# Attention with a fourth score bank, and the maxima in two slots of 1024 and 512 columns

## What is computed

```python
# in the feed-forward block, twice: T = 2048, 16 heads of 8 channels
scores = jnp.einsum('bqhd,bkhd->bhqk', q, k) / jnp.sqrt(jnp.float32(Dh))
attn = jax.nn.softmax(scores, axis=-1)
ctx = jnp.einsum('bhqk,bkhd->bqhd', attn, v).reshape(Bb, Ss, Dd)
# the latent attention, with weights that are folded to q, k, v first
attn = jnp.where(causal[None, None], attn, -jnp.inf)
attn = jax.nn.softmax(attn, axis=-1)
```

## Time and profile before

| | us |
|---|---|
| median of 3 runs | 3145.35 (3127.97 to 3156.62) |
| the profiled execution, own time | 3132.53 |
| its span, first to last instruction | 3130.8 |
| PE busy | 2834.4 (91%) |
| DVE busy | 1998.1 (64%) |
| ACT busy | 1757.0 (56%) |
| mean granted clock of PE | 0.910 |

### The profile page before, as it was taken

How to read it: one execution, slowest core, us unless ns; L and a number is a source line. 1 busy time by engine, 2 the same in 40 slices (tenths; PEclk the granted TensorE clock), 3 DMA queues, 4 the chain that set the end, 5 groups by cost and what they waited for, 6 DMA issues and landing times. The chain is left out here.

```text
span 3130.8 us, 49981 instructions
## 1 busy us (share of the span) xinstructions
PE 2834.4 (91%) x15208; PEld 1329.6 (42%) x15208; DVE 1998.1 (64%) x2708; ACT 1757.0 (56%) x3373; POOL 260.3 (8%) x488
## 2 busy tenths in 40 slices
PE   6788857999999998999499999958999999998998
PEld 2688853333333333444244444424333333334443
DVE  5544456888888882322567777636888888882222
ACT  4222210788787887443156666631788788786433
POOL 1222202000000000000211111111000000000000
PEclk9888855999999999899679998975999999998999
DMA  1000002111001100211211111111011111000211
GB/s 38 1 0 0 0 1 74 28 28 27 24 17 27 27 21 1 78 44 40 74 28 42 27 41 36 26 54 34 16 27 27 27 27 26 16 20 15 68 60 34
DMA packets 37077, 94.13 MB, mean 30 GB/s; under 512 B 9258, under 2 KB 23044, under 8 KB 28804
## 3 DMA queue, kind: packets, MB, share of 16 engines
q1 hardware_dynamic: 33892, 91.18, 10.8%
q10 hardware_dynamic: 3104, 1.88, 0.2%
HBM read 78.45 MB, written 13.76 MB: 29 GB/s over the span
## 5 line engine op out<-in xcount | busy, mean ns | idle before, releaser
L507 DVE TENSOR_REDUCE Hmaxes<-Hm 128x1 f32<-128x1024 f32 x512 | 603.2, 1219 | 100.4 <-PE Hm L271 99.0
L507 DVE TENSOR_REDUCE Fmaxes<-Fm 128x1 f32<-128x1024 f32 x512 | 603.2, 1219 | 99.8 <-PE Fm L271 98.3
L418 ACT ACTIVATE Hprob<-Hs 128x512 f32<-128x512 f32 x1024 | 528.7, 603 | 117.7 <-PE Hs L283 117.2
L418 ACT ACTIVATE Fprob<-Fs 128x512 f32<-128x512 f32 x1024 | 528.6, 603 | 117.8 <-PE Fs L283 117.3
L283 PE MATMUL Hs<-Hqa,Hka 64*128 64x512 f32 x1024 | 409.4, 467 | 5.6 <-ACT Hprob L418 5.1
L283 PE MATMUL Fs<-Fqa,Fka 64*128 64x512 f32 x1024 | 408.9, 466 | 5.7 <-ACT Fprob L418 5.1
L418 ACT ACTIVATE Lprob<-Ls 128x512 f32<-128x512 f32 (+3 forms) x640 | 301.8, 535 | 135.1 <-PE Ls L283 131.4
L271 PE MATMUL Hm<-Hka,Hqa 64*128 64x512 f32 x1024 | 351.2, 462 | 19.5 <-DMA Hka<-H_kparts 15.9
L271 PE MATMUL Fm<-Fka,Fqa 64*128 64x512 f32 x1024 | 350.6, 460 | 19.2 <-DMA Fka<-F_kparts 15.6
L271 PEld LDWEIGHTS Hm<-Hka,Hqa 64*128 64x128 f32 x1024 | 162.6, 195 | 277.2 <-DVE Hmaxes L507 253.2
L271 PEld LDWEIGHTS Fm<-Fka,Fqa 64*128 64x128 f32 x1024 | 162.3, 195 | 276.7 <-DVE Fmaxes L507 252.8
(11 more groups left out here) (450 smaller groups left out, 2962.6 us busy)
## 6 DMA issues: line engine op xcount, KB each, us to landing
Fqa<-F_qparts SPq DMA_DIRECT2D x64, 128.0 KB
Fka<-F_kparts SPq DMA_DIRECT2D x64, 128.0 KB
FEwb<-FE_weights SPq DMA_DIRECT2D x8, 1024.0 KB, 5.9
Lqa<-L_qparts SPq DMA_DIRECT2D x64, 128.0 KB
Lka<-L_kparts SPq DMA_DIRECT2D x64, 128.0 KB
Hqa<-H_qparts SPq DMA_DIRECT2D x64, 128.0 KB
Hka<-H_kparts SPq DMA_DIRECT2D x64, 128.0 KB
HEwb<-HE_weights SPq DMA_DIRECT2D x8, 1024.0 KB, 5.9
```

Of the source, the lines that this page charges most:

```text
L418: nc.scalar.activation(prob[:, kt % PSLOTS, q0:q1], seat(kt, n)[:, 0:q1 - q0], ACT.Exp, scale=SCALE).then_inc(expd, 1)
L507: nc.vector.reduce_max(maxes[:, qt, half:half + 1], mps[j % 2][:, 0:width], AX.X)\
```

## The change

PSUM's eight banks are divided anew. The ring of scores has four banks in place of three (`HIGH_SLOTS`). The slots for maxima are no longer two of 1024 columns but one of 1024 and one of 512 (`LOW_WIDTHS`), three banks in place of four. Items still alternate between the two slots, and an item is now as wide as its slot, or as the keys that are left. So a full attention has 48 items per head (16 of 1024 and 32 of 512 columns) and the causal one 32; the number of items is kept even by splitting the last one. `EARLY` goes to 12 items in both. A head's entries of the ring (66 and 42) are no multiple of four, so a seat depends on the parity of the head, and ACT's loop runs over pairs of heads.

```diff
-EARLY_FULL, EARLY_CAUSAL = 8, 9
+EARLY_FULL, EARLY_CAUSAL = 12, 12
+HIGH_SLOTS = 4
+LOW_WIDTHS = (2 * BANK, BANK)
...
-    MAXES = [(qt, half, min(2 * BANK, keys(qt) - 2 * BANK * half))
-             for qt in range(NT) for half in range(2) if keys(qt) > 2 * BANK * half]
+    MAXES = []
+    for qt in range(NT):
+        k0 = 0
+        for n in range(NB):
+            if k0 < keys(qt):
+                width = min(LOW_WIDTHS[len(MAXES) % 2], keys(qt) - k0)
+                MAXES.append((qt, n, k0, width))
+                k0 += width
+    if len(MAXES) % 2:
+        qt, n, k0, width = MAXES.pop()
+        MAXES += [(qt, n, k0, width - 2 * P), (qt, n + 1, k0 + width - 2 * P, 2 * P)]
...
-        return offset % 3
+        return offset % HIGH_SLOTS
...
-        maxes = sbo("maxes", [P, NT, 2], F32)
+        maxes = sbo("maxes", [P, NT, NB], F32)
...
-                    sp.sem_inc(expd, 3)
+                    sp.sem_inc(expd, HIGH_SLOTS)
...
-            sps = [ctx.enter_context(nc.psum_tensor(f"{name}s{i}", [P, BANK], F32)) for i in range(3)]
-            mps = [ctx.enter_context(nc.psum_tensor(f"{name}m{i}", [P, 2 * BANK], F32)) for i in range(2)]
+            sps = [ctx.enter_context(nc.psum_tensor(f"{name}s{i}", [P, BANK], F32)) for i in range(HIGH_SLOTS)]
+            mps = [ctx.enter_context(nc.psum_tensor(f"{name}m{i}", [P, w], F32)) for i, w in enumerate(LOW_WIDTHS)]
...
-            def seat(kt, n=0):
+            def seat(u, kt, n=0):
 
-                return ring(AHEAD[kt] + n + (kt > OUT_AFTER) + (kt > TURN_AT))
+                return ring(u * NE + AHEAD[kt] + n + (kt > OUT_AFTER) + (kt > TURN_AT))
...
-                        qt, half, width = MAXES[j]
+                        qt, _, k0, width = MAXES[j]
...
-                        k0 = 2 * BANK * half + n * BANK
+                        k0 += n * BANK
...
-                    head(0, first=True)
-                    with act.Fori(1, NH) as h:
-                        head(h)
+                    head(0, 0, first=True)
+                    head(1, 1)
+                    with act.Fori(1, NH // 2) as i:
+                        for u in range(2):
+                            head(i * 2 + u, u)
```

More of the change, by code:

```diff
@@ L100, in slot_of @@
     def slot_of(offset):
[L101 removed]
+        return offset % HIGH_SLOTS
     stream = [(1, j) for j in range(EARLY, NM)] + [(2, j) for j in range(EARLY)]
[L104 removed]
+    done = np.cumsum([120 + MAXES[j][3] for _, j in stream])
     length = np.cumsum([T - first_query(kt) + 300 * len(blocks(kt)) + (1500 if causal else 0) for kt in range(NT)])
@@ L282, in score @@
                         pe.wait_ge(expd, entry(h, kt, n) + 1)
-                        nc.tensor.matmul(seat(kt, n)[:, 0:q1 - q0], ka[0:LOW, s, kt * P:(kt + 1) * P],
+                        nc.tensor.matmul(seat(s, kt, n)[:, 0:q1 - q0], ka[0:LOW, s, kt * P:(kt + 1) * P],
                                          qa[0:LOW, s, q0:q1], start=True, stop=True).then_inc(scored, 1)
                     def weigh(h, s, kt):
-                        pe.wait_ge(expd, 3 + entry(h, kt, len(blocks(kt)) - 1) + 1)
+                        pe.wait_ge(expd, HIGH_SLOTS + entry(h, kt, len(blocks(kt)) - 1) + 1)
                         if causal:
@@ L325, in deliver @@
                         for j in range(NB):
-                            last = nc.tensor.transpose(ring(OUT_SEAT)[:, j * P:(j + 1) * P],
+                            last = nc.tensor.transpose(out_seat(u)[:, j * P:(j + 1) * P],
                                                        osb[:, j * P:(j + 1) * P] if source is None else source, ident)
@@ L339, in low_item @@
                     def low_item(h, i, s, j):
-                        for n in range(-(-MAXES[j][2] // BANK)):
+                        for n in range(-(-MAXES[j][3] // BANK)):
                             maxima(h, i, s, j, n)
@@ L358, in head @@
                             items = [(ahead, j) for ahead, j in share[kt] if ahead <= rest]
-                            low = [(ahead, j, n) for ahead, j in items for n in range(-(-MAXES[j][2] // BANK))]
+                            low = [(ahead, j, n) for ahead, j in items for n in range(-(-MAXES[j][3] // BANK))]
                             high = len(blocks(kt))
@@ L370, in head @@
                             if kt == OUT_AFTER:
-                                deliver(h, source=ident if first else None)
+                                deliver(h, u, source=ident if first else None)
                             if kt == TURN_AT:
-                                turn(turn_entry(h), TURN_SEAT, h + 2 if rest else h + 1)
+                                turn(turn_entry(h), turn_seat(u), h + 2 if rest else h + 1)
                     head(0, 0, first=True)
@@ L411, in _, with head @@
                                              ACT.Copy).then_inc(expd, 1)
-                    def head(h, first=False):
+                    def head(h, u, first=False):
                         for kt in range(NT):
@@ L491, in item @@
                     def item(h, j):
-                        qt, half, width = MAXES[j]
+                        qt, n, k0, width = MAXES[j]
                         taken = dve.to_reg(h * NM + j + 1)
                         reduced = dve.to_reg(h) if j == 0 and not (isinstance(h, int) and h == 0) else None
-                        if causal and 2 * BANK * half + width == keys(qt):
+                        if causal and k0 + width == keys(qt):
                             dve.wait_ge(filled, FILLED)
@@ L504, in item @@
                                 scale=1.0, scalar=LEAST, op0=ALU.add, op1=ALU.max,
-                                accum_out=maxes[:, qt, half:half + 1]).then_inc(max_free, 1)
+                                accum_out=maxes[:, qt, n:n + 1]).then_inc(max_free, 1)
                         else:
-                            nc.vector.reduce_max(maxes[:, qt, half:half + 1], mps[j % 2][:, 0:width], AX.X)\
+                            nc.vector.reduce_max(maxes[:, qt, n:n + 1], mps[j % 2][:, 0:width], AX.X)\
                                 .then_inc(max_free, 1)
```

28 lines of the change are left out of this document (15 added, 13 removed).

## The result

The changed kernel took 3466.2 us (median of 4 runs, 3455.1 to 3468.1), against 3143.1 us for the kernel before (median of 4): ratio 1.102, 95% interval 1.099 to 1.105. 3450 was forecast, within 3370 to 3600. The profiled execution has a span of 3466.3 us, 335.5 more than before.

| stage, first piece of maxima to last output copy | before | after | difference | forecast |
|---|---|---|---|---|
| first full attention | 493.6 to 1239.6 | 494.7 to 1370.2 | 129.5 | 139 |
| causal attention | 1541.1 to 2067.1 | 1671.8 to 2275.5 | 77.7 | 41 |

The account below looks back on a forecast made before the run. It took full attention to be bound by a 2.61 us loop closed by the third score bank. To the profiled 3132.5 us it added 278 (two full attentions) and 41 (causal), 319: 3451.5, called 3450, range 3370 to 3600.

Parts of the forecast that it names:

- The loop W, S0, exp0, S3, W: Full attention before: weigh block, first score, its exponential, last score, next weigh block; closed by third score bank, 2.61 us.
- The last head: Full attention steps without maxima: fourth score bank takes the exponential out of the loop, 2.22 us, gaining 0.39 each.
- The steady steps: Full attention steps with maxima: waits for a slot make them 3.55 and 2.79 us, plus 0.56 on average.
- The prologue: Full attention, head 0's maxima before the first score: 6.63 us per two query tiles against 5.06, 12.6 us more.
- The causal stage: Causal attention as a whole: 41 us longer, bounds -20 to +90.
- The two stalls: Causal attention, key tiles kt 5 and 8: a 1024 item meets a third item on its slot, plus 1.7 us each.
- 2.6 us per head: Causal attention: net of the steps' losses and gains per head, over some 14.5 heads, 38 us.
- rival 1: Full attention: PE's clock falls in a third of 472 steps, 193 us more, so 3645 us; chance 0.14.
- Rival 2: Full attention: slot waits are hidden and steps fall to DVE's own 2.46 us, total 3065 us; chance 0.04.
- Rival 3: Causal attention: gains 20 us rather than losing, as uneven steps let stalls merge, total 3390 us; chance 0.10.

Follow-up runs that it names:

- causal_3banks: Kernel before, with only the causal attention given maxima slots of 1024 and 512 columns, keeping three score banks; 3247.3 us, ratio 1.035.
- three_slots: Changed kernel with old causal division; full attentions with three score banks and three maxima slots (1024, 512, 512 columns); 3139.5 us, ratio 1.002.
- full_3banks: Changed kernel with old causal division and three score banks in the full attentions, one bank unused; 3415.5 us, ratio 1.089.
- full_only: Changed kernel with the causal attention put back to the old division; 3402.6 us, ratio 1.084 to the kernel before.
- w_early: full_only with the weigh block issued ahead of each step's last piece of maxima and last score; 3258.4 us, ratio 1.041.
- tail4_dummy: Kernel before, with last-head scores borrowing an idle maxima bank, plus useless matmuls ahead of some causal scores; 3157.0 us, ratio 1.004.
- tail4: Kernel before, with ACT's loop over head pairs and last-head scores borrowing an idle maxima bank as fourth; 3126.6 us, ratio 0.9975.

## Why the prediction was right, and where it was off

**The bound before.** The loop W, S0, exp0, S3, W closed by the third score bank was right: with a fourth bank and no maxima the step falls from 2.61 to 2.13 us. Two steps of the tail in the changed kernel:

```profile
1341.88 1.06 PE L322 MATMUL Fo<-Fprob,Fvh 128*32 128x512 f32 x8
1342.88 1.20 PE L297 MATMUL Fs<-Fqa,Fka 64*128 64x512 f32 x4
1344.01 1.06 PE L322 MATMUL Fo<-Fprob,Fvh 128*32 128x512 f32 x8
```

The forecast had 2.22 there: S0 to S3 go out faster than the 0.80 taken, so that W starts 1.13 after S0 and the step is 2.13, ACT's 2.07 close under it. The last head gained 7.1 us where 6.2 were counted (16 x 0.39).

**The steady steps.** 3.55 and 2.79 us were worked out, 3.56 and 2.78 measured, from M-to-DVE, hand-over, reduction and W of the old timeline. The head grew by 8.8 us (42.7 to 51.5) where 16 x 0.56 = 9.0 was said. What remains of the 9.5 and 12.4 us that the full attentions stayed below 139 is mostly in the heads done once: head 0 grew by some 5.5 us and head 1 by 7.5 instead of 9.0, head 14 by 2.5 instead of some 5. The prologue, from the first piece of maxima to the first score, takes 58.4 us before and 73.7 and 71.0 after, plus 15.2 and 12.6 where 15 was counted. Its reductions in the changed kernel repeat every 6.64 us, against the 6.63 in the forecast:

```profile
496.00 1.82 DVE L523 TENSOR_REDUCE Fmaxes<-Fm 128x1 f32<-128x1024 f32 x2 [16.06 <-PE Fm L285]
...
502.64 1.82 DVE L523 TENSOR_REDUCE Fmaxes<-Fm 128x1 f32<-128x1024 f32 x2 [0.71 <-PE Fm L285]
```

**The causal stage** was mis-sized: 77.7 us for 41, though within its bounds of -20 to 90. The two stalls were there as worked out. kt 5 of a head in the changed kernel:

```profile
1913.76 0.50 PE L285 MATMUL Lm<-Lka,Lqa 64*128 64x512 f32 x1
...
1914.33 0.39 PE L285 MATMUL Lm<-Lka,Lqa 64*128 64x512 f32 x1
1915.81 0.39 PE L285 MATMUL Lm<-Lka,Lqa 64*128 64x256 f32 x1 [1.08 <-DVE Lmaxes L523]
...
1917.04 0.50 PE L285 MATMUL Lm<-Lka,Lqa 64*128 64x512 f32 x1
```

1917.04 less 1913.76 is 3.28 us, 3.3 in the forecast; kt 8 takes 3.33 (1920.21 to 1923.54), 3.2 in the forecast. The step that failed is the term "2.6 us per head": it held the stalls, less the gain of the fourth bank, and left PE's clock where it was. Over the same twelve heads the mean went from 30.1 to 36.1 us, 6.0 more. By the estimate at equal clock above, some 2.4 to 2.8 of them are what the term was for, around its 2.6, and 3.2 to 3.6 are the clock, which fell from 0.93 to 0.80 in these heads and was priced at nothing. The clock had been seen falling once per head and was put into rival 1, but for the full attentions; the causal stage, where the fall was already in the rows, got none of it. Two windows of the changed kernel, one head each:

```profile
1903.80:1937.40 33.60, 28.56 (x204) 13.49 (x204) 22.80 (x49) 20.08 (x43) 5.32 (x19) 0.91 0.14 33
2008.90:2047.10 38.20, 34.15 (x204) 15.37 (x204) 23.01 (x49) 20.28 (x43) 5.32 (x19) 0.72 0.12 28
```

Same instructions, 33.6 us at 0.91 and 38.2 at 0.72. So what rival 1 named, a lower clock where PE waits for slots, did come, but in the causal stage and not in the full attentions.

**The rivals.** Rival 1 as stated, for the full attentions, is refuted: PE is empty for 1.08 and 0.31 us per pair of steps and the granted clock stays at 1.00 (first windows of this part of the document). The Trainium skill, "TensorE: Matmul & The Clock Gate", section "A second HAM failure mode: psum-queue depth-cycling", describes a kernel with bf16 matmuls of 512 columns, which cycles through PSUM banks and whose small PE gaps make the clock swing; in this kernel the causal stage does the like (0.92 before, 0.83 after) and the full attention does not (1.00). Rival 2 (waits hidden, 3065 us) fell with the slot free at 2.05 us into the step; even the early weigh block only halved the loss. Rival 3 (causal stage gains) was right that the fourth bank gives something there, 30 us by causal_3banks against the changed kernel, but the stalls and the clock took more.

The Trainium skill, "Perfetto Trace Analysis", section "Matmuls", asks for rotation through different PSUM banks. The runs show both halves of it in numbers, for the first full attention: a bank less for the maxima takes 139 us (three_slots 747.2, full_3banks 886.0), a bank more for the scores then brings 13 back (full_only 872.7), 9.3 of them in the last two heads.

## What to carry to other kernels

Count the pieces that PE issues for a consumer between two long blocks of other work (here four pieces of maxima between two W), and give the ring at least that much room. One bank less put a wait for a reduction into PE's queue, 1.08 us with a slot of 1024 columns and 0.3 us with slots of 512, and everything behind it waited too. If a slot must be reused early, put other long work of PE between the two uses (w_early got back 144 of some 260 us that way). A spare buffer can be lent where its owner has finished: the fourth score bank in the last head alone gave 0.7%, without taking anything from the maxima.

## What the runs showed of the hardware that was not expected

- Useless matmuls made a kernel faster: 55 us (3247 to 3192) where they filled waits and kept the granted clock at 1.00 instead of 0.82; 35 us slower (3122 to 3157) where they stood in front of scores.
- Idle time on PE did not tell where the clock would fall: the full attention, where PE is busy 566 of 725 us, stayed at 1.00, and the causal stage, where it is busy 454 of 517, had 0.83. What sets it stays open. The loads of the next q and k, which run beside the falls (DMA share 0.39 and 0.58 in the windows of tail4_dummy), do not bring them about by themselves: at 854 to 863 us of the kernel before their share is 0.36 to 0.50 and the clock 1.00.
- The last causal head, with identical instructions, took 24.8 to 26.5 us in four profiled executions, at a mean clock of 0.90 to 0.99, and 39.0 us in four others, at 0.50 or 0.51. The steady heads of a full attention repeat to 0.1 us meanwhile.
- Writing two ACT heads out instead of looping cost 0.8 us at the first one (42.7 to 43.5), and the like at the last but one in tail4.
